# Attention in a graph network: softmax reciprocals repeated by VectorE and turned by two transposes per two units, in place of four column-half matmuls

## Time and profile before

| | |
|---|---|
| Runs | 1133.88, 1135.50, 1138.69 us; median 1135.5 us |
| Span of the profiled execution | 1133.4 us (no other time of it is given) |
| Mean granted TensorE clock | 0.981 of full speed |
| TensorE busy / weight loads busy | 1052.5 us (93%) / 689.2 us (61%) |
| VectorE busy | 583.0 us (51%) |
| ACT busy | 445.4 us (39%) |
| GpSimd busy | 157.7 us (14%) |
| Window stage | about 54 to 214 us of the span |
| Attention stage | about 452 to 768 us of the span |

### The profile page before, as it was taken

One profiled execution on the slowest core, in us unless ns is written; L12 is line 12 of the kernel. 1 busy time (PEld: TensorE's weight loads), 2 busy tenths in 40 slices (PEclk: granted clock), 3 DMA queues, 4 the chain that ended last, 5 costly groups with the idle time before them and its releaser, 6 DMA issues.

```text
span 1133.4 us, 16827 instructions
## 1 busy us (share of the span) xinstructions
PE 1052.5 (93%) x5904; PEld 689.2 (61%) x5904; DVE 583.0 (51%) x1743; ACT 445.4 (39%) x762; POOL 157.7 (14%) x182
## 2 busy tenths in 40 slices
PE   6988878899999999899999999999899998999998
PEld 3456656555444554677777777774456896555443
DVE  7888998610884011666665666655447337300133
ACT  6502565400645101565555656552436415410000
POOL 0000000000053000333333000005537012000000
PEclk9999998899999999999999999999999999999999
DMA  5003788850100000554544100026001051100010
GB/s 169 1 0 106 221 259 269 261 178 1 40 35 1 19 19 31 177 152 150 152 140 144 42 1 1 2 82 245 0 1 47 1 192 36 38 1 1 10 46 35
DMA packets 73097, 93.63 MB, mean 83 GB/s; under 512 B 7169, under 2 KB 63176, under 8 KB 73022
## 3 DMA queue, kind: packets, MB, share of 16 engines
q1 hardware_dynamic: 73022, 92.62, 26.1%
HBM read 58.00 MB, written 34.60 MB: 82 GB/s over the span
## 4 chain that ended last, share of the span: by engine, by line
PE 79%; DVE 10%; issue 5%; ACT 4%; DMA 1%; SPq 1%; DVEq 0%; ACTq 0%
PE PS L557 8%; PE PS L788 8%; PE PS L590 8%; PE PS L771 8%; PE PS L936 7%; PE PS L743 7%; PE PS L971 6%; PE PS L714 5%; PE PS L613 5%; PE PS L529 2%; DVE R L1241 2%; PE PS L700 2%; DVE HT L1106 2%; PE PS L891 2%; PE PS L918 2%
## 5 line engine op out<-in xcount | busy, mean ns | idle before, releaser
L557 PE MATMUL PS<-HT,R 125*128 125x313 bf16 x636 | 130.5, 351 | 27.0 <-DVE HT L1106 15.8
L1230 DVE CUSTOM_DVE_ANT_0 HT<-PS,CD 128x1250 f32<-128x1250 f32 (+1 forms) x80 | 116.4, 1455 | 67.4 <-issue 67.4
L557 PEld LDWEIGHTS PS<-HT,R 125*128 x636 | 98.0, 172 | 59.9 <-issue 45.4
L771 PE MATMUL PS<-K,HT 128*128 128x128 f32 (+2 forms) x800 | 112.5, 280 | 15.0 <-DVE R L1241 14.4
L1535 ACT COPY R<-PS 128x512 f32<-128x512 f32 (+1 forms) x120 | 64.8, 574 | 121.5 <-PE PS L771 119.5
L1555 ACT ACTIVATE HT<-HT,soft 128x1250 f32<-128x1250 f32 (+1 forms) x80 | 107.1, 1338 | 10.3 <-DVE soft L1233 3.3
L771 PEld LDWEIGHTS PS<-K,HT 128*128 128x128 f32 (+2 forms) x800 | 84.0, 140 | 43.2 <-DVE R L1241 23.6
L743 PE MATMUL PS<-R 64*128 64x512 f32 (+3 forms) x480 | 95.8, 531 | 3.1 <-DVE soft L1230 3.1
L788 PE MATMUL PS<-R 128*64 128x128 f32 (+2 forms) x1600 | 94.2, 273 | 0.0
L788 PEld LDWEIGHTS PS<-R 128*64 128x64 f32 (+1 forms) x1600 | 84.8, 137 | 6.4 <-issue 5.8
L590 PE MATMUL PS<-CD,H 128*128 128x512 f32 (+2 forms) x240 | 86.0, 520 | 2.4 <-ACT X L1445 2.4
(11 more groups left out here) (222 smaller groups left out, 1386.2 us busy)
## 6 DMA issues: line engine op xcount, KB each, us to landing
edge_parts<-X SPq DMA_DIRECT2D x160, 156.5 KB, 2.7
R<-edge_parts SPq DMA_DIRECT2D x60, 156.5 KB, 2.3
CD<-edge_sums SPq DMA_DIRECT2D x1, 6250.0 KB, 20.8
CD<-edge_parts SPq DMA_DIRECT2D x10, 469.5 KB, 3.8
BC<-edge_parts SPq DMA_DIRECT2D x30, 156.5 KB, 2.5
CD<-edge_parts SPq DMA_DIRECT2D x3, 1565.0 KB, 10.8
edge_sums<-R SPq DMA_DIRECT2D x20, 156.5 KB, 2.8
R<-edge_parts SPq DMA_DIRECT2D x18, 155.5 KB, 2.3
```

Of the source, the lines that this page charges most:

```text
L557: return mm(bank(b0 + h, QUART), stat, hot, start=first, stop=True, skip_group_check=True)
L771: m = nc.tensor.transpose(PS[0:rows(j), o:o + n], Pb[u % 2][a][0:n, j * P:j * P + rows(j)], ident[0:n, 0:n])
L1230: ve.tensor_tensor_reduce(Pb[s][a][0:n], PS[0:n, a * N:(a + 1) * N], cd[0:n, t, :], 1.0, -3e38, ALU.add, ALU.max, soft[0:n, s, a:a + 1]).t ...
```

## The change

`rz` after L1219 is 128 x 4. Before, L1221 wrote it back as 128 x 4, and four matmuls (two units b, two heads a) spread it. After, L1221 reads it with a broadcast and writes `rzw`, 128 x 256, each of the four columns repeated 64 times; two transposes of 128 x 128 (one for each b) then write the same PSUM area. `rzw` lies in the buffer BC, behind the parts that GpSimd adds up. The semaphores and their counts stay as they were.

The same diff makes the window table 16-bit without sign (it was 32-bit with sign). So that all numbers stay positive, 16384 is added to the chunk numbers in the table and taken off again in the address arithmetic.

```diff
+U16 = mybir.dt.uint16
+SHIFT = 16384
@@
-        winI = BC[0:1, 1200:1200 + NG * VALUES].bitcast(I32)
+        winI = BC[0:1, 1200:1200 + NG * VALUES].bitcast(U16)[:, 0:NG * VALUES]
@@
+        rzw = BC[:, 1200:1200 + 4 * DK]
@@ fixed_chunk, late_chunk
-            return bass.ds((d + m + (q - FIX)).with_bounds(min_val=q, max_val=NC - FIX - 1 + q), 1)
+            return bass.ds((d + m + (q - FIX - SHIFT)).with_bounds(min_val=q, max_val=NC - FIX - 1 + q), 1)
@@
-            return bass.ds((d + m).with_bounds(min_val=FIX, max_val=NC - 1), 1)
+            return bass.ds((d + m + -SHIFT).with_bounds(min_val=FIX, max_val=NC - 1), 1)
@@ spread_norms (TensorE)
                 for b in range(2):
-                    for a in range(2):
-                        o = RZ + b * P
-                        i = mm(PS[a * DK:(a + 1) * DK, o:o + n],
-                               rz[0:n, 2 * b + a:2 * b + a + 1].to_broadcast([n, DK]), ident[0:n, 0:n], start=True,
-                               stop=True, skip_group_check=True)
+                    i = nc.tensor.transpose(PS[:, RZ + b * P:RZ + b * P + n], rzw[0:n, b * P:(b + 1) * P], ident[0:n, 0:n])
                 i.then_inc(sem("a_ps"), 1)
@@ the table (VectorE)
-                    link(ve.tensor_scalar(ends, ends, 1.0 - FIX, None, ALU.add))
+                    link(ve.tensor_scalar(ends, ends, 1.0 - FIX - SHIFT, None, ALU.add))
@@ the reciprocals (VectorE)
-                    ve.tensor_scalar(rz[0:n], rz[0:n], hasedge[0:n, t:t + 1], None, ALU.mult).then_inc(sem("z_ready"), 1)
+                    ve.tensor_scalar(rzw[0:n].rearrange("p (h d) -> p h d", d=DK), rz[0:n].unsqueeze(2).to_broadcast([n, 4, DK]),
+                                     hasedge[0:n, t:t + 1], None, ALU.mult).then_inc(sem("z_ready"), 1)
```

## The result

| | before | after |
|---|---|---|
| Median of the runs | 1134.7 us (6 runs, 1130.5 to 1138.7) | 1180.8 us (6 runs, 1179.6 to 1183.0) |
| Span of the profiled execution | 1133.4 us | 1179.4 us |
| Ratio | | 1.042, 95% interval 1.039 to 1.044 |

The change makes the kernel 46 us slower, 4.2%. The forecast was 1132.0 us, with a range of 1127 to 1138. In the attention, which the change is about, a pair of units became shorter almost exactly as forecast.

What follows compares the result with a forecast made beforehand. TensorE, busy 93% of the span, was taken as the bound in most stages. Transposes for matmuls -4.5, wider multiply 0, address arithmetic +1.0, loads 0: 1135.5 - 3.5 = 1132.0 us, range 1127 to 1138.

Steps and rivals of the forecast that it cites:

- Part 5: Window stage, register loads of 20 numbers on both queues: price per number, so 2-byte numbers change the time by 0.
- Rival (d): L252 on TensorE's queue, nine times: 2-byte register loads take longer; doubled, +16.5 us in all, 1152.0 us; chance 0.07.
- Parts 1 and 2: Attention loop: L800's matmuls removed, two transposes added per pair of units; together -4.5 us.
- The sign named for it: Between L788 and L771 loads: 2 records instead of 8, about 0.21 us instead of 0.44 on the chain.
- Rival (c): Attention transposes cost the quoted 275 ns each: +2.2 us, with +1.0 of arithmetic 1138.7 us; chance 0.05.
- Part 3: VectorE's wider multiply L1221: 0.23 us grows to about 0.42, covered by L1230's wait, so cost 0.
- Part 4: Window stage addresses gain a subtraction of 16384: 15 ns a step, showing in 39 extra trips, +1.0 us.
- rival (b): Window stage: the added address step shows in all 632 records, +9.5 us, giving 1140.5 us; chance 0.13.
- The sum: Whole kernel: -4.5 + 0 + 1.0 + 0 = -3.5 us.

Runs made afterwards that it cites:

- old-spread: Three traces of kernels whose spread is still four matmuls from the 4-wide product; mean distance across the attention 333.7 us.
- new-spread: Ten traces of kernels whose spread is done by transposes; mean distance across the attention 329.2 us.
- word tables: Against the changed kernel: 4-byte signed window table, no 16384, trip's end and-ed with 65535, transposes kept; 1132.2 us, ratio to before 0.997.
- The word table with the 16384: 4-byte signed table, and with 65535, transposes kept, 16384 added in the table and subtracted in the address; 1132.2 us, ratio to before 0.9973.
- the and: Trip's end and-ed with 65535 in a register; the kernel before with only this (4-byte signed table, four-matmul spread) took 1139.1 us, ratio 1.0023.
- the and made once: 4-byte signed table with transposes, the and with 65535 made once behind the load instead of in each trip; 1137.4 us, ratio to before 1.001.

## Why the prediction was wrong, and where it was right

**Part 5 failed** ("I take the price to be per number, so 0"): the cost of the loads was put at nothing, and it was 50 us. The price of about 0.1 us a word holds for adjacent words from a 16-byte border, and for nothing else that was tried. All others cost 4.9/20 = 0.25 us in the first load, when no DMA ran, and about 7.5/20 = 0.37 us later: 2-byte numbers, words apart and words off the border. On TensorE's queue the ten loads took 71.7 us in place of 21.3, and the window stage ended 50.4 us later. The text said that no row showed a 2-byte load, but it gave a factor of two as the dear end and 7 chances in 100. Rival (d) had the place and the mechanism right (2-byte loads take longer, and TensorE stands idle for them nine times in the stage). That VectorE would stand still too it didn't say. Its size, double and 20 us, was a guess; the nine loads grew 3.4-fold, by 47 us. The range stopped at 1138 because rival (d)'s chance was put in the part left out; with a duration that no row showed, it should not have been.

The Trainium skill, "Runtime: NRT & Kernel Launch", Instruction fetch mechanics, gives about 200 ns a register for this instruction (TENSOR_LOAD), which that page describes as a load from HBM. Here the table lies in SBUF, and the first load's numbers cost 0.25 us each where they weren't adjacent words on a border. The trace before showed half of the page's figure for words; the right question would have been what the words do to get below it. A price per register alone would still have left Part 5 at 0.

**Parts 1 and 2 were right.** The pair of units lasts 15.59 us (15.6 forecast), and the means of the old-spread and new-spread traces differ by 4.5 us (4.5 forecast). The sign named for it came in another form: L802 has 0.37 us on the chain and not 0.21, because it took over the entry cost from L775, whose 0.60 fell to 0.45. Rival (c), 275 ns for each transpose, is out: two more transposes cost 0.22 us, twice their step. One record of a transpose does last that long (mean 278 ns at L775), but records behind each other overlap, so the step between two starts is the price.

**Part 3 was right.** L1221 took 0.35 us, mean 0.38 (0.42 forecast), and VectorE still idles 0.82 us before L1231. TensorE didn't wait for `z_ready` in the chain.

**Part 4: no cost seen, the step misread.** VectorE's fused record for a late address takes 67 ns in place of 55 (70 forecast). On TensorE the late addresses' records rose from 44 or 49 to 53 ns, so the step is under the 15 ns forecast, and the 64 ns that I had read as four steps belong to fixed chunks and are 59 after. The price in time was forecast at 1.0 us; the word tables with and without the step both have 1132.2 us. Their intervals are some 2 us wide to each side, so 0 and 1.0 can't be told apart, but rival (b), 9.5 us, is out.

**The sum** of what it covered was right as far as the runs can tell. The word table with the 16384 is the change without the 2-byte loads and with the and. It is 3.1 us under before, and 5.7 with the and's 2.6 us taken off; the forecast without Part 5 was -3.5, and the uncertainty is over 2 us. The kernel's change consisted of two parts, and the second, which the change's own words didn't name, was ten times the first.

## What to carry to other kernels

Register loads from SBUF stalled the queues of both engines here, so they belong in the sum like matmuls do: lay what is loaded together as adjacent 4-byte words, start it on a multiple of 16 bytes, and don't make the numbers smaller to save bytes. Before pricing a load (or anything) by an average over many elements, ask whether the elements came together, and whether the new form still lets them. And an edit of types or constants beside the edit that a change is named after has to be priced with as wide a bound as it: where no row shows the operation, keep the far end inside the range.

## What the runs showed that I had not expected

- The time of a register load follows where its numbers lie. Twenty numbers take 1.35 to 2.7 us as adjacent words from a 16-byte border, and 4.7 to 8.6 us as 2-byte numbers, as every second word, or as adjacent words starting 4 bytes off. Ten words starting 8 bytes off took 2.3 to 4.95 us, from a border 1.06 to 2.8 us. How many words come together at a time isn't settled. A group of four, counted from the load's start, would fit: five groups in about 2.1 us and two groups and two single words in 1.6 us are both about 0.4 us apiece, an estimate from these medians.
- The same load is slower with DMA traffic beside it: 4.9 us at 52 us of the span, where no transfer ran, and 8.6 us at 197 us, where the DMA engines were 0.91 busy. That the traffic is the cause wasn't tried.
- An added step of arithmetic in an address that is computed in a fused record cost nothing that 12 runs can tell, while an and outside the fused records (118 more records of 36 to 40 ns on each queue) cost 2.6 us (interval 0.9 to 4.3).
- The granted clock was lower where the stalls were longer: 0.78 from 84 us to the end of the window stage after, against 0.90 in the earlier trace rows. Runs with about the same stalls also differ (0.93 in the word table, 0.89 with the and made once), so the stalls aren't all of it.
